# Cross-attention and feed-forward kernel: queries' and output's products on scaled 16-bit planes

## The chip, the cores and the metric

The kernel runs on one core of a Trainium2 chip. Its time is the device time in microseconds of one execution, as the median of several runs. A core has five engines that run side by side and meet at semaphores: TensorE (PE, matrix products; PEld is its loading of the stationary operand), VectorE (DVE), ScalarE (ACT), GpSimd (POOL), and SyncE (SP), which here issues every DMA. Sixteen DMA engines move the data. SBUF is the working memory of 128 partitions; TensorE writes its results into PSUM, eight banks of 512 fp32 columns.

## What is computed

Two layers, each an attention-like part and a feed-forward part, on x (2 batches x 512 tokens x 1024) and a context ctx (2 x 1024 x 1024), in float32:

```
x += fake_quant(layernorm(x)) @ fake_quant(ctx)          # 8-bit levels, layer 0
h  = layernorm(x)
x += h @ W.T + b + 2 * lora(h, routing from the mean of h)
h  = layernorm(x)                                        # layer 1
q  = rope(h @ wq)      32 heads x 128
k, v = rope(ctx @ wk), ctx @ wv      8 heads x 128, each used by 4 query heads
x += softmax(q k / sqrt(128) + mask) v @ wo
h  = layernorm(x)
x += h @ W_up.T + lora of the expert that the gate picks
```

The products have to be close to float32. The kernel gets this from two planes: a value is stored as a high plane (rounded to the narrower type) and a low plane (value minus high plane), and a product is three: low x high, high x low, high x high (`mm3`, lines 42 to 45).

## The kernel before

All five engines have a program written out by hand, in fixed order; each instruction waits for semaphores that name the step it needs. An engine never runs ahead of an instruction that waits. The names in the trace are tiles; the lines are those of the kernel before.

**First stage, 0 to about 408 us.** In 64 steps `s` TensorE makes keys and values of both batches, 24 products of 512 columns a step, and between them layer 0's quantised product. VectorE and ScalarE finish each step, SP stores planes of k and v to scratch in HBM. ScalarE's work in a step ends with the copy of planes and, in some steps, the root for a layernorm.

**Second stage, about 408 to 545 us.** The feed-forward of layer 0 in tiles of 128 tokens, a layernorm for each tile (`layernorm`, L1175: VectorE's statistics, ScalarE's root at L1679, VectorE again), the transposes of h through PSUM (`h_turn`), its high plane by ScalarE (`h_hi`, L1729) and low plane by VectorE (`h_lo`, L1371), stored by SP to `h_scratch` and read back transposed as hTa, hTb, hTc (1 MB each part, fp32).

**Third stage, the loop over heads, p = 0 to 65, each with four windows w.** The 64 heads are 32 heads of two batches. In a window TensorE does a quarter of the next head's queries (`q_part`, 6 products), scores of one tile of 128 queries (`scores`, 6), a quarter of the output product of the head pair before (`wo_part`, 6), and in window 0 also the values' product of the head before (`values`, 24, from 16-bit planes pT and vsb). The order in a window is values, q_part, wo_part, scores; in window 0 the output part comes after the scores. Planes of the queries' and output's products are fp32 planes of reduced precision (F32R, 4 bytes): wqh, wql, hT, woh, wol, osb.

What the others do in a window: VectorE makes `p_lo` of one tile (L1524: two inputs in SBUF), the row scale, the addition of the output product to x (`wo_add`, L1540), the maximum of the scores (L1507); in window 0 the low plane of the head's output (`o_lo`, L1529). After window 3 it applies the rope to the next queries (`q_end`, L1499). ScalarE makes the exponential (L1846), the high plane of the probabilities (`p_hi`, L1853), the cast of one slice of weights (`split_w`, L1805), in window 0 the cast of the head's output (`o_hi`, L1861), after window 3 that of the queries (`q_hi`, L1839). GpSimd has the low plane of the same slice (`split_w`, L1996) and the sum and low plane of the queries (`q_lo`, L2000 and L2002). SP issues the four loads of slices of the iteration (`load_w`, L601, 256 KB each, into four slots, each freed by the subtraction L1996), and in each window a transposing DMA of probabilities (`turn_p`, L625). `p_hi` of a tile waits for the transpose of the tile three before.

The first output product of an even p needs `o_lo` of the head before, the one just computed (L1022):

```
            if i == 0:
                e.wait_ge(p_wlo.sem, p_wlo[W_AT["o", q, 1]])
                e.wait_ge(v_olo.sem, v_olo[2 * j + 1])
```

Of the kernel before, what the change touches and what calls it, by code (L numbers as in the profile page):

```python
# [103 lines left out]
W_SLOT = [n % 4 if n < 250 else 2 + n % 2 for n in range(len(W_ORDER))]  # L104
# [6 lines left out]
UP_ON_DVE = [2, 3]  # L111
UP_LOAD_AT = {(62, 0): 0, (62, 1): 1, (62, 2): 2, (62, 3): 3, (63, 0): 4, (63, 3): 5, (64, 0): 6, (64, 1): 7}


def build_in(nc, ctx, A, out):
# [10 lines left out]
    h_d = nc.dram_tensor("h_scratch", [2, 128, 4, 2, 2, 512], F32, kind="Internal").ap()  # L126
# [15 lines left out]
    vsc = alloc(ctx, "vsc", [128, 24])  # L142

    x_lo = alloc(ctx, "x_lo", [128, 4, 1024])
# [11 lines left out]
    t_sb = alloc(one, "t_sb", [128, 512])  # L156
    khl = alloc(one, "khl", [128, 2, 2, 512], F32R)
# [27 lines left out]
    hTb = alloc(two, "hTb", [128, 4, 2, 2, 128], F32R)  # L185
    woh = alloc(two, "woh", [128, 2, 2, 512], F32R)
# [7 lines left out]
    osb = alloc(two, "osb", [128, 3, 2, 512], F32R)  # L194
    hTc = alloc(two, "hTc", [128, 4, 2, 2, 128], F32R)
# [102 lines left out]

    def w_dst(key, hl):
# [78 lines left out]
    t_rt = signal("t_rt", range(2))  # L378
# [25 lines left out]
    v_h2 = signal("v_h2", range(8))  # L404
    v_rt = signal("v_rt", [(b, j) for b in range(2) for j in range(8)])
# [26 lines left out]
    a_h2 = signal("a_h2", range(8))  # L432
    a_rt = signal("a_rt", range(2))
# [20 lines left out]
    p_qlo = signal("p_qlo", heads)  # L454
    v_up = signal("v_up", UP_ON_DVE)
# [5 lines left out]
    d_const = {n: signal(f"d_{n}", [n], 16) for n in ("cosk", "sink", "identf", "identb", "onesb", "scal", "bias", "rw",  # L461
                                                      "rb", "cosq", "sinq", "ag", "lb", "eb")}
# [6 lines left out]
    d_ar = [signal(f"d_ar{r}", [n for n in range(len(W_ORDER)) if W_SLOT[n] == r], 16) for r in range(4)]  # L469
# [5 lines left out]
    d_r3 = [signal(f"d_r3{r}", [k for k in range(8) if UP_SLOT[k] == r], 16) for r in range(3)]  # L475
# [26 lines left out]
    def sync_program(e):  # L502
# [21 lines left out]
        load("cosk", cosk[:, :])  # L524
        load("sink", sink[:, :])
# [8 lines left out]
        load("onesb", onesb[:, :])  # L534
        for group in steps():
# [55 lines left out]
        def store_h(tile):  # L591
            b, i = tile // 4, tile % 4
            for j in range(2):
                e.wait_ge(v_klo.sem, v_klo[tile, j])
                e.dma_start(h_d[b, :, i, j, :, :], f32(khl[:, j, :, :])).then_inc(d_khl[j].sem, 16)

        def load_w(key):
# [3 lines left out]
            e.dma_start(araw[:, W_SLOT[n], :], w_src(key)).then_inc(d_ar[W_SLOT[n]].sem, 16)  # L601

        def load_h(b, w):
            e.wait_ge(d_khl[w // 2].sem, d_khl[w // 2]["h", 4 * b + 3])
            e.dma_start(f32(hT_part(w)), h_d[b, :, :, w // 2, :, w % 2 * 256:w % 2 * 256 + 256].rearrange(
# [42 lines left out]

        e.wait_ge(t_kv.sem, t_kv[63])
        weights_split(e)  # L650
        for n in range(4):
            load_w(("q", n))
        for i in range(4):
            store_h(i)
            if i == 1:
# [8 lines left out]
        store_h(4)  # L664

# [15 lines left out]
        load("cosq", cosq[:, :])  # L681
        load("sinq", sinq[:, :])
# [15 lines left out]
        for p in range(66):  # L698
            if p % 4 == 0:
                load_k(p // 4 + 1)  # L700
            if 0 < p and 2 * p + 6 < 128:
                load_w(("q", 2 * p + 6))
            if has_wo(p + 1) and p < 62:
                load_w(("o", p + 1, 0))
                load_w(("o", p + 1, 1))
            if 0 < p and 2 * p + 7 < 128:
                load_w(("q", 2 * p + 7))
            for w in range(4):
# [8 lines left out]
                if 61 <= p <= 63 and w == 2:  # L717
                    load_w(("o", p + 2, 0))
                    load_w(("o", p + 2, 1))
# [44 lines left out]
    def tensor_program(e):  # L764
# [65 lines left out]

        def ffn_turn(tile):
# [17 lines left out]
        def router_end(b):  # L849
            e.wait_ge(v_rt.sem, v_rt[b, 2])  # L850
            if b == 0:
                e.wait_ge(d_const["rw"].sem, 16)
                e.wait_ge(d_const["rb"].sem, 16)
# [8 lines left out]
        for group in steps():  # L862
# [8 lines left out]
            if s in FFN_TURN_AT:  # L871
                ffn_turn(FFN_TURN_AT[s])
        def lora_t(b):
# [142 lines left out]
        def wo_part(q, i):  # L1016
# [145 lines left out]
    def vector_program(e):  # L1162
# [12 lines left out]
        def layernorm(key, x, dst):  # L1175
# [25 lines left out]
        def kv_end(s):  # L1201
# [907 lines left out]
```

## Time and profile before

| | us |
|---|---|
| median of 3 runs (lowest, highest) | 2078.19 (2078.07, 2079.86) |
| profiled execution, first to last instruction (span) | 2076.3 |
| around the span, to the median | 1.9 |
| mean granted TensorE clock | 0.997 of full speed |

The runs have no time of the profiled execution apart from its span, so the difference between span and median stands for what lies around it.

The page's second part cuts the span into 40 slices of 52 us; each digit is a busy share in tenths:

```profile
PE   8999999999899999999999999999999999999899
DVE  5887786667678877878878788888787877878744
ACT  3432341222365655565555555565555555655400
POOL 1552362511133343443434433334344343342400
```

TensorE is at nine tenths in nearly all of them. Slices 1 to 8 are the first stage, 9 to 11 the second and the start of the heads, 12 to 37 the loop. VectorE runs at seven to eight tenths in the loop. In the rows further down, a line such as "1000.33 0.39 PE L45 MATMUL" has the start, the duration, the engine, the line of the kernel and the operation; then output and inputs, shapes and types, and in brackets the idle time before it with what ended it. Matmuls overlap, so the time between two starts is the pace, not the duration.

### The profile page before, as it was taken

The numbers are of one execution on the slowest core, as the hardware profiler recorded it, in microseconds if no ns is written. First come the engines' busy times: TensorE is split into PE (matmuls) and PEld (weight loads), VectorE is DVE, ScalarE is ACT, GpSimd is POOL, SyncE is SP. The second block draws the span as 40 slices with busy tenths as digits, with TensorE's granted clock in tenths as the row PEclk, the third lists the DMA queues.
The fourth block names the chain that finished last, engine by engine and source line by source line (L and its number), as shares of the span: only waits on it lengthen the run. The fifth ranks groups of instructions, "written<-read, shape, count | busy, mean of one in ns | idle before, by whom it ended". The sixth has DMA issues, their size and how long they took to land.

```text
span 2076.3 us, 25530 instructions
## 1 busy us (share of the span) xinstructions
PE 2023.1 (97%) x9112; PEld 1520.3 (73%) x9116; DVE 1575.3 (76%) x2880; ACT 1002.6 (48%) x1418; POOL 747.1 (36%) x495
## 2 busy tenths in 40 slices
PE   8999999999899999999999999999999999999899
PEld 6877777887667777777777776777777777777587
DVE  5887786667678877878878788888787877878744
ACT  3432341222365655565555555565555555655400
POOL 1552362511133343443434433334344343342400
PEclk9999999999999999999999999999999999999999
DMA  7543553312978688786887899878687786777712
GB/s 267 171 162 122 186 170 102 133 60 101 325 173 172 140 185 168 148 178 137 190 165 146 198 237 235 192 149 184 141 181 165 151 183 142 172 161 142 206 61 72
DMA packets 654942, 341.11 MB, mean 164 GB/s; under 512 B 574720, under 2 KB 591360, under 8 KB 652768
## 3 DMA queue, kind: packets, MB, share of 16 engines
q1 hardware_dynamic: 654816, 339.48, 67.9%
q8 instruction: 73, 1.20, 0.2%
q14 instruction: 53, 0.43, 0.1%
HBM read 152.76 MB, written 44.04 MB: 95 GB/s over the span
## 4 chain that ended last, share of the span: by engine, by line
PE 78%; DVE 6%; DMA 3%; issue 2%; POOL 2%; ACT 1%; SPq 1%; DVEq 0%; ACTq 0%; POOLq 0%
PE ps L43 26%; PE ps L45 25%; PE ps L44 25%; DMA pT<-pp 1%; PE ps L820 1%; POOL u_sb L1960 1%; DVE t_sb L1164 1%; DVE pp L1524 1%; DVE psb L1507 1%; DMA raw<-in_ctx 0%; SPq L625 0%; DMA sinq<-in_sinq 0%; PE ps L1060 0%; PE ps L1044 0%; PE ps L827 0%
## 5 line engine op out<-in xcount | busy, mean ns | idle before, releaser
L1846 ACT ACTIVATE psb<-psb,st 128x1024 f32<-128x1024 f32 x256 | 295.1, 1153 | 220.7 <-DVE st L1510 220.5
L1524 DVE SCALAR_TENSOR_TENSOR pp<-psb,st,pp 128x1024 f16<-128x1024 f32 x256 | 380.9, 1488 | 5.1 <-ACT pp L1853 3.0
L1507 DVE CUSTOM_DVE_ANT_0 psb<-ps,mask 128x1024 f32<-128x1024 f32 x256 | 313.5, 1224 | 84.7 <-PE ps L45 77.9
L1853 ACT ACTIVATE pp<-psb,st 128x1024 f16<-128x1024 f32 x256 | 293.7, 1147 | 144.9 <-DVE st L1519 143.8
L1996 POOL TENSOR_TENSOR wol<-araw,woh 128x512 fp32r<-128x512 f32 x128 | 167.6, 1310 | 431.9 <-ACT woh L1805 431.8
L1996 POOL TENSOR_TENSOR wql<-araw,wqh 128x512 fp32r<-128x512 f32 x128 | 165.3, 1292 | 331.6 <-ACT wqh L1805 331.6
L1164 DVE TENSOR_TENSOR x_lo<-ps,x_lo 128x512 f32<-128x512 f32 x264 | 181.0, 686 | 51.8 <-PE ps L45 51.8
L43 PE MATMUL ps<-woh,osb 128*128 128x512 f32 x512 | 202.6, 396 | 9.3 <-DVE x_lo L1164 4.1
L43 PE MATMUL ps<-ksb,qsb 128*128 128x512 f32 x512 | 200.5, 392 | 7.5 <-DVE st L1507 4.5
L44 PE MATMUL ps<-wol,osb 128*128 128x512 f32 x512 | 200.2, 391 | 0.0
L45 PE MATMUL ps<-woh,osb 128*128 128x512 f32 x512 | 200.2, 391 | 0.0
L45 PE MATMUL ps<-ksb,qsb 128*128 128x512 f32 x512 | 199.5, 390 | 0.0
L43 PE MATMUL ps<-pT,vsb 128*128 128x512 f16 x512 | 194.8, 380 | 4.9 <-DMA pT<-pp 4.9
L44 PE MATMUL ps<-ksb,qsb 128*128 128x512 f32 x512 | 199.5, 390 | 0.0
L45 PE MATMUL ps<-pT,vsb 128*128 128x512 f16 x512 | 194.1, 379 | 0.0
L44 PE MATMUL ps<-pT,vsb 128*128 128x512 f16 x512 | 194.1, 379 | 0.0
L43 PE MATMUL ps<-slots,wl 128*128 128x512 f32 x448 | 177.8, 397 | 11.4 <-ACT slots L1659 8.3
L45 PE MATMUL ps<-slots,wh 128*128 128x512 f32 x448 | 175.4, 392 | 0.0
L44 PE MATMUL ps<-slots,wh 128*128 128x512 f32 x448 | 175.1, 391 | 0.0
L2000 POOL TENSOR_TENSOR ua<-ua,ta 128x512 f32<-128x512 f32 x64 | 136.5, 2133 | 82.2 <-DVE ta L1164 82.2
L1839 ACT CAST qsb<-ua 128x512 fp32r<-128x512 f32 x64 | 39.7, 620 | 193.5 <-POOL ua L2000 193.5
L1529 DVE SCALAR_TENSOR_TENSOR osb<-ps,vsc,osb 128x512 fp32r<-128x512 f32 x64 | 48.1, 751 | 111.5 <-ACT osb L1861 111.5
(254 smaller groups left out, 4131.2 us busy)
## 6 DMA issues: line engine op xcount, KB each, us to landing
araw<-in_wq SPq DMA_DIRECT2D x128, 256.0 KB, 4.8
araw<-in_wo SPq DMA_DIRECT2D x128, 256.0 KB, 4.5
k_scratch<-khl SPq DMA_DIRECT2D x32, 512.0 KB, 3.6
ksb<-k_scratch SPq DMA_DIRECT2D x16, 1024.0 KB, 6.0
raw<-in_wv SPq DMA_DIRECT2D x16, 512.0 KB, 4.5
raw<-in_ctxT SPq DMA_DIRECT2D x16, 512.0 KB, 4.6
raw<-in_wk SPq DMA_DIRECT2D x16, 512.0 KB, 5.6
raw<-in_ctx SPq DMA_DIRECT2D x16, 512.0 KB, 4.6
```

Of the source, the lines that this page charges most:

```text
L43: e.matmul(dst, ll, rh, start=start, stop=False)
L44: e.matmul(dst, lh, rl, start=False, stop=False)
L45: return e.matmul(dst, lh, rh, start=False, stop=stop)
L1164: return e.tensor_tensor(dst, a, b, op)
L1507: e.tensor_tensor_reduce(out=psb[:, n % 3, :], in0=pair(n % 2 * 2), in1=mask[:, i, :], scale=1.0, scalar=LOWEST, op0=ALU.add, op1=ALU.max, ...
L1524: e.scalar_tensor_tensor(out=pp[:, r, 1024:2048], in0=psb[:, r, :], scalar=st[:, n // 4 % 4, 16 + i:17 + i], in1=pp[:, r, 0:1024], op0=ALU ...
L1529: e.scalar_tensor_tensor(out=osb[:, H % 3, 1, :], in0=bank(4), scalar=vsc[:, H // 4:H // 4 + 1], in1=f32(osb[:, H % 3, 0, :]), op0=ALU.mul ...
L1839: e.copy(qsb[:, H % 2, 0, :], ua[:, :]).then_inc(a_qhi.sem, 1)
L1846: e.activation(P, P, ACT.Exp, bias=c[:, 4 + i:5 + i], accum_out=c[:, 8 + i:9 + i]).then_inc(a_exp.sem, 1)
L1853: e.activation(pp[:, r, 0:1024], psb[:, r, :], ACT.Copy, scale=st[:, n // 4 % 4, 16 + i:17 + i]).then_inc(a_ph.sem, 1)
L1996: e.tensor_tensor(w_dst(key, 1), araw[:, W_SLOT[n], :], f32(w_dst(key, 0)), ALU.subtract).then_inc(p_wlo.sem, 1)
L2000: e.tensor_tensor(ua[:, :], ua[:, :], ta[:, :], ALU.add).then_inc(p_qu.sem, 1)
```

## The change

- The planes of queries' and output's products (wqh, wql, hT, woh, wol, osb) become float16. The tiles keep their places in SBUF.
- Float16 has a small range, so weights are scaled by a power of two first. The power comes from the sum of squares of all of wq and of all of wo. 128 slices of 512 columns are loaded ahead of time (`load_square`, SP), squared and summed by ScalarE (`square`), added over partitions by three small fp32 products (`square_sums`, TensorE), and turned into scales by short chains on VectorE (`query_sums`, `query_scale`, `value_squares`, `output_sums`, `output_scales`). 64 slices (wq) fall into steps 6 to 59 of the first stage, 64 (wo) into the second stage, between ScalarE's pieces there.
- GpSimd multiplies every raw slice by its scale in place (`scale_w`), called one slice ahead at the start of `split_w`; ScalarE's cast waits for that.
- Raw slices get eight slots instead of four, and are loaded one iteration earlier. At p = 0 SP now has four loads ahead of the first `turn_p` of the loop, where it had none.
- cosq and sinq are multiplied by the inverse scale before the first rope, the layernorm of h by 1024, and the addition of the output product multiplies it by its inverse scale.
- Some semaphores of constants are shared, and h_scratch has half its bytes.

The core of the diff:

```
-W_SLOT = [n % 4 if n < 250 else 2 + n % 2 for n in range(len(W_ORDER))]
+W_SLOT = [n % 4 if n < 8 else n % 8 if n < 248 else 2 + (n - 248) % 6 for n in range(len(W_ORDER))]
+SQUARE_STEPS = sorted([*range(6, 28), *range(38, 60), *range(40, 60)])
+H_SCALE = 1024.0
...
-    wqh = alloc(two, "wqh", [128, 3, 512], F32R)
-    wql = alloc(two, "wql", [128, 3, 512], F32R)
+    wqh = alloc(two, "wqh", [128, 3, 512], F16)
+    alloc(two, "wqh_pad", [128, 1536], F16)
+    wql = alloc(two, "wql", [128, 3, 512], F16)
+    alloc(two, "wql_pad", [128, 1536], F16)
...
+        def load_square(n):
+            if n > 6:
+                e.wait_ge(a_sq.sem, a_sq[n - 7])
+            w = A["wq" if n < 64 else "wo"][n // 2 % 32]
+            e.dma_start(scan[:, n % 7, :], w[:, n % 2 * 512:n % 2 * 512 + 512]).then_inc(d_scan[n].sem, 16)
...
         for p in range(66):
             if p % 4 == 0:
                 load_k(p // 4 + 1)
-            if 0 < p and 2 * p + 6 < 128:
-                load_w(("q", 2 * p + 6))
-            if has_wo(p + 1) and p < 62:
-                load_w(("o", p + 1, 0))
-                load_w(("o", p + 1, 1))
-            if 0 < p and 2 * p + 7 < 128:
-                load_w(("q", 2 * p + 7))
+            if 2 * p + 8 < 128:
+                load_w(("q", 2 * p + 8))
+            if p < 64:
+                load_w(("o", p + 2, 0))
+                load_w(("o", p + 2, 1))
+            if 2 * p + 9 < 128:
+                load_w(("q", 2 * p + 9))
...
+        def square_sums(what):
+            if what == "w":
+                e.wait_ge(v_scal.sem, v_scal[0])
+                e.wait_ge(a_sq.sem, a_sq[63])
+                e.wait_ge(v_l0.sem, v_l0[1, 6, 0])
+                e.matmul(ps[:, 7, 0:64], twos[:, :], squares[:, 0:64], start=True, stop=True).then_inc(t_rt.sem, 1)
+            else:
+                e.wait_ge(a_sq.sem, a_sq[127])
+                e.wait_ge(v_ws.sem, v_ws["v", 1])
+                e.wait_ge(v_qr.sem, v_qr[0])
+                e.matmul(ps[:, 7, 0:64], twos[:, :], squares[:, 64:128], start=True, stop=True)
+                e.matmul(ps[:, 7, 64:80], twos[:, :], sc[:, 32:48], start=True, stop=True).then_inc(t_rt.sem, 1)
...
+        def query_sums():
+            e.wait_ge(t_rt.sem, t_rt["w"])
+            e.tensor_reduce(sc[:, 0:1], ps[:, 7, 0:64], AX, ALU.add).then_inc(v_ws.sem, 1)
+            bound(1, "w", 0)
...
         split_lo("c21")
+        query_sums()
+        query_scale()
         row_sums(1)
...
+                e.tensor_scalar(cosq[:, :], cosq[:, :], sc[:, 18:19], None, ALU.mult).then_inc(v_ws.sem, 1)
+                e.tensor_scalar(sinq[:, :], sinq[:, :], sc[:, 18:19], None, ALU.mult).then_inc(v_ws.sem, 1)
...
-            tt(xs, bank(6 + i % 2), xs, ALU.add).then_inc(v_xa.sem, 1)
+            e.scalar_tensor_tensor(out=xs, in0=bank(6 + i % 2), scalar=sc[:, 30 + (q - 2) // 32:31 + (q - 2) // 32], in1=xs,
+                                   op0=ALU.mult, op1=ALU.add).then_inc(v_xa.sem, 1)
...
+                if (p, w) == (0, 1):
+                    output_sums()
+                    output_scales()
...
+        def square(n):
+            e.wait_ge(d_scan[n].sem, d_scan[n]["s", n])
+            e.activation(scan[:, n % 7, :], scan[:, n % 7, :], ACT.Square, accum_out=squares[:, n:n + 1]).then_inc(a_sq.sem, 1)
...
         ffn_hi(4)
+        for n in range(72, 75):
+            square(n)
         root(("f", 6))
...
+        ffn_hi(5)
+        for n in range(76, 84):
+            square(n)
+        root(("f", 7))
         split_w(("q", 0))
...
+        for n in range(125, 128):
+            square(n)
         split_w(("q", 3))
...
+        def scale_w(n):
+            if n < len(W_ORDER):
+                wo, r = W_ORDER[n][0] == "o", W_SLOT[n]
+                e.wait_ge(d_ar[r].sem, d_ar[r][n])
+                if n == 0:
+                    e.wait_ge(v_ws.sem, v_ws["w", 5])
+                if wo and n < 12:
+                    e.wait_ge(v_ws.sem, v_ws["v", 8])
+                e.tensor_scalar(w_raw(n), w_raw(n), sc[:, 16 + wo:17 + wo], None, ALU.mult).then_inc(p_ws.sem, 1)
+
         def split_w(key):
             n = W_AT[key]
+            scale_w(n + 1)
             e.wait_ge(a_whi.sem, a_whi[n])
-            e.tensor_tensor(w_dst(key, 1), araw[:, W_SLOT[n], :], f32(w_dst(key, 0)), ALU.subtract).then_inc(p_wlo.sem, 1)
+            e.tensor_tensor(w_dst(key, 1), w_raw(n), w_dst(key, 0), ALU.subtract).then_inc(p_wlo.sem, 1)
```

## Rows read from the trace of the kernel before

**Rows 1.** The page, busy us (share of the span) xinstructions:
```profile
PE 2023.1 (97%) x9112; PEld 1520.3 (73%) x9116; DVE 1575.3 (76%) x2880; ACT 1002.6 (48%) x1418; POOL 747.1 (36%) x495
```
**Rows 2.** Busy time by stretch: us, then each engine, clock, DMA:
```profile
640.00:1900.00 1260.00, 1253.70 (x5556) 912.64 (x5555) 1011.98 (x1852) 735.99 (x1042) 500.98 (x346) 1.00 0.80 171
```
**Rows 3.** TensorE in order of time, a 32-bit run, then values' products:
```profile
1000.33 0.39 PE L45 MATMUL ps<-hTb,wqh 128*128 128x512 f32 x1
...
1007.13 0.39 PE L45 MATMUL ps<-ksb,qsb 128*128 128x512 f32 x1
...
1007.59 0.38 PE L44 MATMUL ps<-pT,vsb 128*128 128x512 f16 x1
...
1012.12 0.38 PE L44 MATMUL ps<-pT,vsb 128*128 128x512 f16 x1
```
**Rows 4.** TensorE, last scores product and first output product of an even p:
```profile
1079.69 0.39 PE L45 MATMUL ps<-ksb,qsb 128*128 128x512 f32 x1
1080.20 0.47 PE L43 MATMUL ps<-woh,osb 128*128 128x512 f32 x1
```
**Rows 5.** All engines in order of time, ahead of that output product:
```profile
1075.65 1.28 DVE L1524 SCALAR_TENSOR_TENSOR pp<-psb,st,pp 128x1024 f16<-128x1024 f32 x1
...
1075.70 2.38 POOL L2000 TENSOR_TENSOR ua<-ua,ta 128x512 f32<-128x512 f32 x1 [1.14 <-DVE ta L1164]
...
1078.63 0.68 ACT L1861 ACTIVATE osb<-ps,vsc 128x512 fp32r<-128x512 f32 x1
...
1079.35 0.75 DVE L1529 SCALAR_TENSOR_TENSOR osb<-ps,vsc,osb 128x512 fp32r<-128x512 f32 x1 [2.15 <-ACT osb L1861]
```
**Rows 6.** The same view, windows 2 and 3 of the iteration before:
```profile
1063.86 1.29 POOL L1996 TENSOR_TENSOR wol<-araw,woh 128x512 fp32r<-128x512 f32 x1 [3.16 <-ACT woh L1805]
...
1065.36 1.27 DVE L1524 SCALAR_TENSOR_TENSOR pp<-psb,st,pp 128x1024 f16<-128x1024 f32 x1
...
1068.87 1.30 POOL L1996 TENSOR_TENSOR wol<-araw,woh 128x512 fp32r<-128x512 f32 x1 [3.72 <-ACT woh L1805]
...
1069.44 1.81 DVE L1524 SCALAR_TENSOR_TENSOR pp<-psb,st,pp 128x1024 f16<-128x1024 f32 x1
```
**Rows 7.** Groups by line: xcount, busy us, mean ns, idle before:
```profile
L1996 POOL TENSOR_TENSOR wql<-araw,wqh 128x512 fp32r<-128x512 f32 x128 | 165.3, 1292 | 331.6 <-ACT wqh L1805 331.6
...
L1164 DVE TENSOR_TENSOR x_lo<-ps,x_lo 128x512 f32<-128x512 f32 x264 | 181.0, 686 | 51.8 <-PE ps L45 51.8
...
L1529 DVE SCALAR_TENSOR_TENSOR osb<-ps,vsc,osb 128x512 fp32r<-128x512 f32 x64 | 48.1, 751 | 111.5 <-ACT osb L1861 111.5
...
L1839 ACT CAST qsb<-ua 128x512 fp32r<-128x512 f32 x64 | 39.7, 620 | 193.5 <-POOL ua L2000 193.5
...
L1679 ACT ACT_TABLE_LOAD x4 | 5.1, 1283 | 0.1
```
**Rows 8.** All engines in order of time, first stage:
```profile
74.25 2.96 DVE L1197 TENSOR_SCALAR tmp<-x_lo,sm 128x1024 f32<-128x1024 f32 x1
74.28 2.39 POOL L1952 TENSOR_TENSOR wl<-raw,wh 128x1024 fp32r<-128x1024 f32 x1
```
**Rows 9.** SP's issues, GpSimd and ScalarE in order of time, p = 0:
```profile
564.21 15.95 SPq L625 DMA_TRANSPOSE pT<-pp  x4
...
572.03 1.89 POOL L1996 TENSOR_TENSOR wql<-araw,wqh 128x512 fp32r<-128x512 f32 x1 [4.32 <-ACT wqh L1805]
...
575.71 1.15 ACT L1853 ACTIVATE pp<-psb,st 128x1024 f16<-128x1024 f32 x1
```
**Rows 10.** DMA issues, 640 to 1900 us: count, median us to landing:
```profile
pT<-pp SPq DMA_TRANSPOSE x232, 4.3
```
**Rows 11.** A small VectorE operation; ScalarE's root ahead of tile 7:
```profile
397.62 0.15 DVE L1228 TENSOR_SCALAR vsc<-vsc 128x1 f32<-128x1 f32 x1
...
473.28 0.20 ACT L1679 ACTIVATE sm<-sm 128x1 f32<-128x1 f32 x1 [8.15 <-DVE sm L1183]
```
**Rows 12.** TensorE in order of time, start of the second stage:
```profile
415.17 0.47 PE L43 MATMUL ps<-slots,h2s 128*128 128x512 f32 x1 [1.61 <-DVE slots L1164]
```

More of the change, by code:

```diff
@@ L111 @@
 UP_ON_DVE = [2, 3]
+SQUARE_STEPS = sorted([*range(6, 28), *range(38, 60), *range(40, 60)])
+SQUARE_LOAD_STEP = [max(SQUARE_STEPS[n - 7] + 1 if n > 6 else 0, SQUARE_STEPS[n] - 2) for n in range(64)]
+SQUARES = range(128)
+H_SCALE = 1024.0
 UP_LOAD_AT = {(62, 0): 0, (62, 1): 1, (62, 2): 2, (62, 3): 3, (63, 0): 4, (63, 3): 5, (64, 0): 6, (64, 1): 7}
@@ L142, in build_in @@
     vsc = alloc(ctx, "vsc", [128, 24])
+    vso = alloc(ctx, "vso", [128, 16])
+    twos = alloc(ctx, "twos", [128, 128])
+    squares = alloc(ctx, "squares", [128, 128])
+    sc = alloc(ctx, "sc", [128, 64])
+    more = ExitStack()
+    araw2 = alloc(more, "araw2", [128, 4, 512])
+    more.close()
+    scan = alloc(ctx, "scan", [128, 7, 512])
     x_lo = alloc(ctx, "x_lo", [128, 4, 1024])
@@ L404, in build_in @@
     v_h2 = signal("v_h2", range(8))
+    v_ws = signal("v_ws", [("w", j) for j in range(7)] + [("v", j) for j in range(2)] + ["cosq", "sinq"]
+                  + [("v", j) for j in range(2, 12)])
     v_rt = signal("v_rt", [(b, j) for b in range(2) for j in range(8)])
@@ L580, in sync_program @@
                 load_raw(f"x{C_LOAD_AT[s]}")
+            for m in range(64):
+                if SQUARE_LOAD_STEP[m] == s:
+                    load_square(m)
         load_raw("c20")
@@ L646, in load_up @@
             e.dma_start(raw3(k), A["up"][k]).then_inc(d_r3[UP_SLOT[k]].sem, 16)
+        for n in range(64, 71):
+            load_square(n)
         e.wait_ge(t_kv.sem, t_kv[63])
@@ L652, in sync_program @@
             load_w(("q", n))
+        for n in range(71, 105):
+            load_square(n)
         for i in range(4):
             store_h(i)
+            for n in (range(105, 110), range(110, 116), range(116, 120), range(120, 125))[i]:
+                load_square(n)
             if i == 1:
@@ new lines, in output_sums, with output_scales @@
+        def output_sums():
+            e.wait_ge(t_rt.sem, t_rt["v"])
+            e.tensor_reduce(sc[:, 0:1], ps[:, 7, 0:64], AX, ALU.add).then_inc(v_ws.sem, 1)
+            e.tensor_reduce(sc[:, 1:3], ps[:, 7, 64:80].rearrange("p (a b) -> p a b", a=2), AX, ALU.add).then_inc(v_ws.sem, 1)
+            bound(3, "v", 3)
+        def output_scales():
+            floor_roots(3, "v", 5)
+            e.tensor_scalar(sc[:, 17:18], sc[:, 12:13], 2.0 ** 14, None, ALU.mult).then_inc(v_ws.sem, 1)
+            e.tensor_scalar(sc[:, 20:22], sc[:, 13:15], 2.0 ** 13, None, ALU.mult).then_inc(v_ws.sem, 1)
+            e.tensor_scalar(sc[:, 30:32], sc[:, 10:12], sc[:, 9:10], 2.0 ** -27, ALU.mult, ALU.mult).then_inc(v_ws.sem, 1)
+            e.wait_ge(v_ws.sem, v_ws["v", 9])
+            for b in range(2):
+                m = e.tensor_scalar(vso[:, 8 * b:8 * b + 8], vsc[:, 8 * b:8 * b + 8], sc[:, 20 + b:21 + b], None, ALU.mult)
+            m.then_inc(v_ws.sem, 1)
@@ L1775, in scalar_program @@
                 root(("f", FFN_NORM_AT[s]))
+            for n in range(64):
+                if SQUARE_STEPS[n] in group:
+                    square(n)
         split_hi("c20")
@@ L1787, in scalar_program @@
         lora_hi(0)
+        for n in range(64, 72):
+            square(n)
         def split_w(key):
             n = W_AT[key]
-            e.wait_ge(d_ar[W_SLOT[n]].sem, d_ar[W_SLOT[n]][n])
+            e.wait_ge(p_ws.sem, p_ws[n])
             if key[0] == "q":
@@ L2004, in gpsimd_program @@
         bias(6)
+        scale_w(0)
         bias(7)
```

154 lines of the change are left out of this document (111 added, 43 removed).

## The prediction

> **What bounds the kernel now.** I read the page first: TensorE is busy 97% of the span, VectorE 76%, ScalarE 48%, GpSimd 36% [rows 1]. Then the busy times by stretch: from 640 to 1900 us, in the loop over heads, TensorE has 1253.7 of 1260 us at granted clock 1.00, VectorE 1012, GpSimd 501 [rows 2]. So the loop, 61% of the time, goes at the pace of matmuls, and an edit counts there if it shortens matmuls or makes TensorE wait. Then TensorE in order of time, start to start: 30 steps of products on 32-bit planes from 1000.33 to 1007.13 us give 0.2267 us each, 21 steps of 16-bit ones (values) from 1007.59 to 1012.12 give 0.2157 [rows 3]. A product of 512 columns is thus 0.0110 us cheaper on 16-bit planes. The durations printed there overlap; I don't use them.
> Last, what TensorE still waits for. An iteration (one head) lasts 21.54 or 21.92 us by turns; the longer one has a wait ahead of its first output product, from 1079.69 to 1080.20 where 0.227 is due, with 0.08 in the next step [rows 4]: 0.37 us, in 26 of the 29 even iterations between 640 and 1900. Its cause stands in four rows [rows 5]: VectorE starts `p_lo` (L1524, two SBUF inputs) at 1075.65, GpSimd starts the query addition (L2000) 0.05 later and takes 2.38 us, 1.1 more than its like in [rows 6]; the query cast waits for that, ScalarE's cast of the head's output stands behind it (1078.63), then VectorE's low plane of the output (1079.35 to 1080.10), then the product. GpSimd and VectorE's operations with two SBUF inputs exclude one another. This chain decides what the change is worth.
>
> **The change part by part.** The sum is made against the profiled execution: span 2076.3, and 1.9 us around it make the median of 2078.2.
> *Matmuls.* 64 heads x 24 of the queries and as many of the output go to 16-bit planes: 3072 x 0.0110 = 33.8 us. The 72 of heads 0 to 2 and the 96 of the last four output steps lie where TensorE waits for others anyway; without them 31.9. The order query, output, scores now changes kind in every window: from 1007.13 to 1007.59 one 32-bit and one first 16-bit step take 0.46 where 0.442 would be due [rows 3]; over all 63 such places I read 0.0115 a change. Three more 16-bit runs in each of 61 iterations lose 183 x 0.0115 = 2.1. Term: -29.8 us (bounds -33.8 and -27).
> *GpSimd's scaling (`scale_w`)*, 252 operations of 128x512, four an iteration. The trace has no GpSimd operation with one tensor input; the nearest is the subtraction with two, 1.29 us [rows 7], the upper bound; the lower is half of it, 0.65, if half the reads are half the time. I take 0.8, nearer the lower, as reads are what differs. As busy time it is free: 3.2 us on an engine busy 8.6 of 21.7. But it stands right behind each subtraction, and `p_lo` comes there. Today, in window 2, the subtraction ends at 1065.15 and `p_lo` starts at 1065.36, unhindered; in window 3 it starts inside the subtraction, takes 1.81 instead of 1.27 and so begins when GpSimd is done [rows 6]. Who goes first when both come at once: with 0.03 us between the stamps GpSimd won, and 0.8 us of VectorE took 2.96 [rows 8]; with 0.05 VectorE won [rows 5]. No row has a second GpSimd operation queued while VectorE waits; I expect VectorE to get in.
> Stepped forward from an output product at 0, with halves of 1.29 and scores of 1.36 us: window 0's subtraction ends at 2.0, scaling at 2.8, `p_lo` is due at 2.2, ends 0.4 late. Window 1's scores end at 5.25, so the next `p_lo` is due at 6.8 in any case; ScalarE, 0.4 late, has let the subtraction run to 7.2: 0.2 late. Window 2: due at 10.7, subtraction to 11.6, 0.65 late, as today. The head's rope starts 0.15 us late. When the race at 2.2 costs 0.9, the same steps give 0.6. Cover ahead of the output product (query and scores products) shrinks by 0.06, so the wait of the even iterations becomes 0.6 to 1.0 us for 0.37. Term: +0.4 x 31 = +12 us (bounds 0 and +44, under the rivals).
> *VectorE in the loop.* The addition of the output product turns into a scaled one: 0.686 now, 0.751 for the like operation with a pointer scalar [rows 7]; 0.065 x 4 an iteration, inside the steps above. ScalarE's casts and all low planes keep their element counts: 0 (bounds -0.1 and +0.1 us each, off the path except for the head's output, +-3 in all).
> *Loads.* Slices come one iteration earlier into eight slots; in the steady loop SP waits for the same subtraction as now: 0. At iteration 0 four loads are new ahead of SP's `turn_p(1)`, issued today at 564.21; the last waits for slice 7's subtraction, ended at 573.9 [rows 9]. The transpose lands 4.3 us [rows 10] after about 575, and `p_hi(4)`, at 575.71 today [rows 9], waits for it, near 4 us. Slices already there take part of this back later on: +1.5. The output's scales add 12 small VectorE operations there, each 0.15 [rows 11] and 0.04 to the next: 2.3 us, of which 1.0 counts.
> *Squares.* 128 loads of 256 KB and 128 ScalarE squares of 512 columns: a cast of that size is 0.62 [rows 7], 0.75 with the sum's read-out, 96 us in all. Up to 408 us they stand last in a step of 5.4 us, one or two each, where ScalarE idles: 0. From 443 to 545 they fill its waits, as eight of them the 8.15 us ahead of the root at 473.28 [rows 11]. +0.5 where they don't fit; if they don't hide, +8.
> *Ahead of the heads.* `query_sums` and `query_scale`, eight small VectorE operations of 0.19, stand before low planes of W's slices, for which TensorE already waits at 415.17 [rows 12]: +1.5. Scaling cosq and sinq +0.9, given back by halved stores of h in the same chain. Three small fp32 products +0.3. This and the two paragraphs before: +5 (bounds -2 and +14).
> Together -29.8 + 12 + 5 = -12.8: 2065.4.
> The Trainium skill (GPSIMD Engine Reference, Engine selection) has one-input operations on GpSimd at roughly line rate, while two-input ones are about twice as slow as VectorE's; no row here shows it. By it `scale_w` would be near 0.6, the +12 near +8, and the sum 2061.
>
> **The rivals.**
> *The port costs nothing:* `p_lo` never loses to a scaling. The wait is 0.37 + 0.06: 2078.2 - 29.8 + 2 + 4 = 2054. For it: GpSimd idles 60% of the loop [rows 2]; against: the 0.21 us between subtraction and `p_lo` [rows 6].
> *Just cancelled:* `scale_w` takes 1.29 like the subtraction. A race is lost in every iteration, the wait becomes 1.0 to 1.1, and a transpose comes 0.1 late to the values: +0.8 x 31 = 25, in all 2078.
> *Slower:* GpSimd keeps the port from subtraction to scaling while VectorE waits. Then `p_lo` loses 0.6 to 1.2 in two or three windows, rope is 1.0 late, the output product waits 1.3, and window 2's transposes reach the values 0.4 and 0.1 late: 1.8 a pair of iterations for 0.37, +1.43 x 31 = 44; 2078.2 - 29.8 + 44 + 5 = 2097. It decides from 1.0 us of extra wait a pair. [Rows 8] speaks for it, the 1.81 in [rows 6] against.
> *The squares don't stay in their cover:* they need another function table than the root. Loads of a table take 1.28 us and stand at changes between root and exponential [rows 7]; with squares between, each of ten roots from 457 to 540 us waits for one, on the path of VectorE's layernorm. Two thirds of 12.8 us reach TensorE: +9, 2074. The Trainium skill (ScalarE: Activation LUTs, Table sets: the hidden batching unit) names relu, copy, identity and abs as part of every set and not the square; by it the loads come if the root's set lacks it.
>
> **How the numbers follow.** Forecast 0.50, port free 0.17, cancelled 0.14, slower 0.12, tables 0.07. The time is the first's, 2065. The range goes from 2048, below the port-free case since GpSimd could also come to win the race of [rows 5] and end today's 0.37 x 26, to 2085, which leaves out the slower case and little else. A measurement can tell 0.2%, 4.2 us, from no change. Faster (under 2074.0): 0.44 of the forecast's 0.50, port free, half of tables: 0.65. Same: the forecast's rest, half of tables, most of cancelled: 0.17. Slower: 0.18.
>
> **What would show it.** Steps of query and output products at 0.216; iterations without a wait at 21.0 us. The wait ahead of the first output product in even iterations: 0.43 is the port-free case, 0.6 to 1.0 mine, 1.3 with waits for pT the slower one. The duration of `scale_w`; how many `p_lo` take 1.27, 1.8 or more; table loads between 443 and 545; when the values' first product starts. I am wrong if 16-bit products beside 32-bit ones don't keep 0.216, or if waits for slices or masks appear.

## The result and the profile after

The changed kernel takes 2065.89 us (median of 5 runs, 2063.38 to 2070.57) where the kernel before took 2078.19 beside it (2078.01 to 2082.31): 0.9945 of it, 95% interval 0.9933 to 0.9958. The forecast was 2065. The profiled execution has a span of 2061.6 against 2076.3, 14.7 us less. That sum came out right although two of its terms were wrong, by about as much in opposite directions.

Two stamps divide the trace: the first product on the second head's values, and that of the 62nd. Columns: start in us, duration, engine, line, operation, tiles, shapes, count, idle time and its releaser. Before:
```profile
594.24 0.38 PE L43 MATMUL ps<-pT,vsb 128*128 128x512 f16 x1 [2.12 <-DMA pT<-pp]
...
1900.32 0.39 PE L43 MATMUL ps<-pT,vsb 128*128 128x512 f16 x1
```
After:
```profile
608.53 0.38 PE L43 MATMUL ps<-pT,vsb 128*128 128x512 f16 x1 [0.73 <-DMA pT<-pp]
...
1886.01 0.39 PE L43 MATMUL ps<-pT,vsb 128*128 128x512 f16 x1
```
The way to the first stamp became 14.3 us longer. The 60 iterations between them take 1277.5 for 1306.1 us, 28.6 less (periods of 21.15 and 21.45 by turns, for 21.54 and 21.93). What is behind takes 175.6 for 176.0.

The page's busy line, which is of the whole span, and the loop's row answer to [rows 1, 2]:
```profile
PE 2001.8 (97%) x9118; PEld 1235.3 (60%) x9122; DVE 1599.0 (78%) x2903; ACT 1080.4 (52%) x1674; POOL 1266.2 (61%) x751
```
```profile
640.00:1900.00 1260.00, 1252.86 (x5675) 665.36 (x5674) 1061.30 (x1895) 752.74 (x1064) 996.29 (x589) 1.00 0.81 172
```
TensorE is as full as before, at the same granted clock of 1.00 (2.4 GHz). GpSimd is busy twice as long, 996 for 501 us, and nobody waits for it more than before. The products of queries and output now go at the 16-bit pace (against [rows 3]): eleven steps from the first row to the second take 2.38 us, 0.216 each, and that is the median step inside these runs over the whole loop, where it was 0.227.
```profile
1000.19 0.38 PE L43 MATMUL ps<-hTa,wql 128*128 128x512 f16 x1
...
1002.57 0.38 PE L45 MATMUL ps<-woh,osb 128*128 128x512 f16 x1
```
The chain ahead of an even iteration's first output product is that of [rows 4, 5], no longer than it was:
```profile
1036.97 1.28 DVE L1658 SCALAR_TENSOR_TENSOR pp<-psb,st,pp 128x1024 f16<-128x1024 f32 x1
1037.02 2.36 POOL L2185 TENSOR_TENSOR ua<-ua,ta 128x512 f32<-128x512 f32 x1 [1.22 <-DVE ta L1239]
...
1040.66 0.75 DVE L1663 SCALAR_TENSOR_TENSOR osb<-ps,vso,osb 128x512 f16<-128x512 f32 x1 [2.14 <-ACT osb L2035]
...
1041.51 0.38 PE L43 MATMUL ps<-woh,osb 128*128 128x512 f16 x1 [0.17 <-issue]
```
18 iterations between 620 and 1890 us have such a step, of 0.56 us where 0.22 is due: 0.34 lost. Before, 26 lost 0.37, the step behind it included. I had forecast 0.6 to 1.0 in 31.

By line, shapes apart (columns: count, busy us, mean ns, idle before), against [rows 7]:
```profile
L2175 POOL TENSOR_SCALAR araw<-araw,sc 128x512 f32<-128x512 f32 x256 | 563.2, 2200 | 51.9 <-DMA araw<-in_wq 51.9
L2181 POOL TENSOR_TENSOR wol<-araw,woh 128x512 f16<-128x512 f32 x128 | 149.0, 1165 | 109.4 <-ACT woh L1953 109.4
...
L1876 ACT ACTIVATE scan<-scan 128x512 f32<-128x512 f32 x128 | 79.3, 624 | 0.0
L1876 ACT ACTIVATION_READ_ACCUMULATOR scan<-scan 128x1 f32 x128 | 24.4, 191 | 0.0
L1817 ACT ACT_TABLE_LOAD x4 | 5.1, 1283 | 0.1
```
The scaling takes 2.20 us, far above my upper bound of 1.29; alone it is 1.56 (91 of 256), in the other cases it stands behind VectorE and is stamped with 2.5 to 2.6. The subtraction went from 1.29 to 1.17 with its 16-bit result. Table loads are four at the root and eight in all, as before: the squares needed none. The Trainium skill (ScalarE: Activation LUTs, Table sets: the hidden batching unit) has relu, copy, identity and abs in every set and doesn't name the square among them; here the square caused no load either, beside root, exponential and copy, and the rival of the table loads fell.

**Where the 14.3 us arise.** The last rope additions of stage 1, before and then after, show that 8.7 of the 14.3 were there already:
```profile
407.77 2.32 POOL L1960 TENSOR_TENSOR u_sb<-u_sb,t_sb 128x512 f32<-128x512 f32 x1 [0.92 <-DVE t_sb L1164]
```
```profile
416.46 2.33 POOL L2134 TENSOR_TENSOR u_sb<-u_sb,t_sb 128x512 f32<-128x512 f32 x1 [0.93 <-DVE t_sb L1239]
```
Of the 8.7, 5.0 had come by the rope addition that was at 297 us before, 2.7 more come by that of 318, none from there to that of 382, and 1.0 at that of 388. One link of the stretch around 300 us, in time order, before:
```profile
298.59 0.62 ACT L1667 CAST khl<-u_sb 128x512 fp32r<-128x512 f32 x1 [5.04 <-POOL u_sb L1960]
299.12 1.05 ACT L1659 CAST wh<-raw 128x1024 fp32r<-128x1024 f32 x1
...
301.99 0.68 DVE L1164 TENSOR_TENSOR u_sb<-ps,cosk 128x512 f32<-128x512 f32 x1
...
307.92 2.13 POOL L1972 TENSOR_TENSOR ctab<-ctab,bq 128x1024 f16<-128x1024 f16 x1
310.10 0.60 PE L807 MATMUL ps<-ctab,onesb 128*128 128x512 f16 x2 [1.41 <-POOL ctab L1972]
```
The same stretch after:
```profile
304.13 0.63 ACT L1805 CAST khl<-u_sb 128x512 fp32r<-128x512 f32 x1 [4.36 <-POOL u_sb L2134]
304.66 0.63 ACT L1876 ACTIVATE scan<-scan 128x512 f32<-128x512 f32 x1
305.29 0.62 ACT L1876 ACTIVATE scan<-scan 128x512 f32<-128x512 f32 x1
305.90 1.04 ACT L1797 CAST wh<-raw 128x1024 fp32r<-128x1024 f32 x1
306.97 1.23 DVE L1239 TENSOR_TENSOR wl<-raw,wh 128x1024 fp32r<-128x1024 f32 x1 [2.32 <-ACT wh L1797]
308.12 0.68 DVE L1239 TENSOR_TENSOR u_sb<-ps,cosk 128x512 f32<-128x512 f32 x1
...
314.01 2.13 POOL L2146 TENSOR_TENSOR ctab<-ctab,bq 128x1024 f16<-128x1024 f16 x1
...
316.19 1.03 PE L863 MATMUL ps<-ctab,onesb 128*128 128x512 f16 x2 [4.90 <-POOL ctab L2146]
```
Two squares stand between the casts. "Last in a step" is first in the next one for an engine that works in order: the weight cast comes 6.8 us after its like of before instead of 5.5, VectorE's low plane waits 2.32 us for it, rope and the context's table follow 6.1 us late, and TensorE waits 4.90 us instead of 1.41. The granted clock falls with it, from 1.00 to 0.91 as the mean of 20 us. Rows of 300 to 320 us, before and then after (columns: window; busy us of PE, PEld, DVE, ACT, POOL, then clock, DMA share, GB/s):
```profile
300.00:320.00 20.00, 18.59 (x89) 14.85 (x88) 14.79 (x27) 6.86 (x11) 9.78 (x6) 1.00 0.47 158
```
```profile
300.00:320.00 20.00, 15.10 (x60) 11.83 (x59) 16.05 (x30) 11.59 (x26) 11.71 (x7) 0.91 0.78 245
```
The second thing to see there is the share of the DMA engines, 0.78 for 0.47.

### The profile page after: what moved, and what is told of

It reads as the page before. It is cut to its first block, busy times and chain, and to the rows that moved or that the text cites. A ratio compares the mean times of both kernels' runs of the same rounds, so it can differ in the third digit from the quotient of the medians.

```text
span 2061.6 us, 26211 instructions
## 1 busy us (share of the span) xinstructions
PE 2001.8 (97%) x9118; PEld 1235.3 (60%) x9122; DVE 1599.0 (78%) x2903; ACT 1080.4 (52%) x1674; POOL 1266.2 (61%) x751
## 4 chain that ended last, share of the span: by engine, by line
PE 77%; DVE 6%; DMA 3%; issue 2%; ACT 2%; POOL 2%; SPq 0%; ACTq 0%; DVEq 0%; POOLq 0%
PE ps L43 25%; PE ps L45 24%; PE ps L44 24%; PE ps L876 1%; POOL u_sb L2134 1%; DMA pT<-pp 1%; DVE t_sb L1239 1%; DMA raw<-in_ctx 1%; DVE pp L1658 1%; DVE psb L1641 0%; DVE vhl_sb L1311 0%; ACT wh L1797 0%; DVE u_sb L1239 0%; PE ps L1133 0%; PE ps L883 0%
## 5 line engine op out<-in xcount | busy, mean ns | idle before, releaser
L2175 POOL TENSOR_SCALAR araw<-araw,sc 128x512 f32<-128x512 f32 x256 | 563.2, 2200 | 51.9 <-DMA araw<-in_wq 51.9
L1658 DVE SCALAR_TENSOR_TENSOR pp<-psb,st,pp 128x1024 f16<-128x1024 f32 x256 | 400.3, 1564 | 3.5 <-ACT pp L2027 1.5
L43 PE MATMUL ps<-ksb,qsb 128*128 128x512 f32 x512 | 250.8, 490 | 9.5 <-DVE st L1641 6.9
L2181 POOL TENSOR_TENSOR wol<-araw,woh 128x512 f16<-128x512 f32 x128 | 149.0, 1165 | 109.4 <-ACT woh L1953 109.4
L43 PE MATMUL ps<-woh,osb 128*128 128x512 f16 x512 | 195.0, 381 | 9.2 <-issue 4.8
L45 PE MATMUL ps<-ksb,qsb 128*128 128x512 f32 x512 | 203.0, 396 | 0.0
L44 PE MATMUL ps<-ksb,qsb 128*128 128x512 f32 x512 | 202.6, 396 | 0.0
L1674 DVE SCALAR_TENSOR_TENSOR x_lo<-ps,sc,x_lo 128x512 f32<-128x512 f32 x256 | 190.4, 744 | 14.0 <-PE ps L45 12.8
L45 PE MATMUL ps<-woh,osb 128*128 128x512 f16 x512 | 194.7, 380 | 0.0
L44 PE MATMUL ps<-wol,osb 128*128 128x512 f16 x512 | 194.5, 380 | 0.0
L2181 POOL TENSOR_TENSOR wql<-araw,wqh 128x512 f16<-128x512 f32 x128 | 149.8, 1170 | 55.3 <-ACT wqh L1953 55.3
L44 PE MATMUL ps<-slots,wh 128*128 128x512 f32 x448 | 175.6, 392 | 0.0
L45 PE MATMUL ps<-slots,wh 128*128 128x512 f32 x448 | 175.6, 392 | 0.0
L2134 POOL TENSOR_TENSOR u_sb<-u_sb,t_sb 128x512 f32<-128x512 f32 x32 | 50.1, 1566 | 153.2 <-DVE t_sb L1239 153.2
```

Of the source, the lines that this page charges most:

```text
L43: e.matmul(dst, ll, rh, start=start, stop=False)
L44: e.matmul(dst, lh, rl, start=False, stop=False)
L45: return e.matmul(dst, lh, rh, start=False, stop=stop)
L1658: e.scalar_tensor_tensor(out=pp[:, r, 1024:2048], in0=psb[:, r, :], scalar=st[:, n // 4 % 4, 16 + i:17 + i], in1=pp[:, r, 0:1024], op0=ALU ...
L1674: e.scalar_tensor_tensor(out=xs, in0=bank(6 + i % 2), scalar=sc[:, 30 + (q - 2) // 32:31 + (q - 2) // 32], in1=xs, op0=ALU.mult, op1=ALU.a ...
L2134: e.tensor_tensor(u, u, t_sb[:, :], ALU.add).then_inc(p_ku.sem, 1)
```

## Experiments

All are compared with the kernel before on the same chip in turn (medians of 2079 to 2080 us there, where it was 2078 beside the result). "Lag" is the start of a stamp less its start in the trace before: at 408 us the last rope addition, at 594 us the second head's values. Each lag is of one trace. Up to 408 us experiments 4, 8 and 12 are the changed kernel, and where that has a lag of 8.7, they have 7.0, 6.8 and 11.2; 8 and 12 are it up to 594 us, too, with 11.5 and 16.3 for 14.3. So a difference of 2 or 3 us between two traces can be scatter. The stretch between the two stamps of the loop is 1277.5 to 1281.2 us in all traces with the change but that of experiment 12. Medians from different chips are best compared by their ratios.

**1. Neither squares nor loads.** `load_square` and `square` do nothing; `squares` is filled with a constant; waits for `a_sq` fall.
```
 def square(n):
-    e.wait_ge(d_scan[n].sem, ...); e.activation(... ACT.Square ...)
+    pass
```


> The changed kernel without the 128 squares on ScalarE and without their 128 loads; the sums that the scales come from are a constant, everything behind them stays. Measured so far: the second head's first value product starts 14.3 us later after the change than before (8.7 us of it by 408 us, while the contexts' keys and values are made). Theory A (squares on ScalarE): ScalarE works in order, and two squares of 0.62 + 0.19 us at the end of a step push its casts and contexts' quantisation; without them 10 to 12 of the 14.3 us go, time 2054 to 2056. Theory B (SP and DMA): the same gain here, but it must come back in the run with loads alone. Theory C (the new small operations ahead of the heads and the scalings): under 3 us go, 2063 or more.

Measured: 2050.53 us, ratio 0.9859 [0.9843, 0.9874]; lag 1.4 us at 408, 2.2 at 594. More came back than I had expected. In the traces the squares and their loads cost 12.1 of the 14.3 us, and all else that the change adds ahead of the second head some 2. Between the medians it is more, as the trace of this run is its slowest execution (2054.77) and that of the changed kernel its fastest (2063.38). The loop is no faster than that after the change (1281.2 us between the stamps).

**2 and 3. Loads alone, squares alone.** In 2 each load waits for the one seven earlier and no square runs. In 3 all squares read one slice.
```
-e.wait_ge(a_sq.sem, a_sq[n - 7])
+e.wait_ge(d_scan[n - 7].sem, d_scan[n - 7]["s", n - 7])        # 2
-e.activation(scan[:, n % 7, :], scan[:, n % 7, :], ACT.Square, ...)
+e.activation(scan[:, 1 + n % 6, :], scan[:, 0, :], ACT.Square, ...)   # 3
```


> The changed kernel with the 128 loads of 256 KB in their places (each waits for the landing of the one seven before, not for its square) but no square on ScalarE; the sums are a constant. Theory A: as without both, 2054 to 2057, and the lag at 408 us under 1.5 us. Theory B (the loads stand ahead of the raw slices' loads on SP, and take the DMA engines): the lag at 408 us stays above 6 us, time 2062 to 2066.

> The changed kernel with its 128 squares on ScalarE in their places, all of one slice loaded once, written into six places by turns; the other 127 loads are left out. Theory A: as the changed kernel, 2063 to 2066, lag at 408 us 7 to 9 us. Theory B: 2054 to 2057, lag under 2 us. If both this and the loads alone keep about half, the two add up: a square waits for its late load and ScalarE stands behind it.

Measured: 2059.17 (0.9895 [0.9879, 0.9911]), lags 6.0 and 8.5; and 2060.10 (0.9900 [0.9885, 0.9915]), lags 5.0 and 9.9. Neither theory alone: with 2050.5 for none and 2065.9 for both, the loads cost 8.7, the squares 9.6, and together 15.4, a little less than the sum. (Experiment 4, on the same chip in turn and with all loads and squares, stands for both at 2065.95.)

**4. No scaling in the loop.** `scale_w` isn't called; the query tables' and output's scales are set to fit.
```
 def split_w(key):
-    scale_w(n + 1)
```


> The changed kernel without GpSimd's 256 scalings of weight slices (2.2 us each as profiled, 563 us of GpSimd): the slices go to 16-bit planes unscaled, and the scales of the query tables and the output are set to fit. Loop from the second to the 62nd head's value products: 1277.5 us with them. Theory A (VectorE gets in between subtraction and scaling, and the delays end inside the cover ahead of the output product): 1275 to 1278 without, time 2062 to 2066. Theory B (my term of +12 is there, and the matmuls gave more than I counted): 1264 to 1267, time 2051 to 2055.

Measured: 2065.95 (0.9927 [0.9913, 0.9940]), the changed kernel's time by the medians and 0.0018 or 3.7 us under it by the ratios, which are as uncertain as that; between the stamps 1281.2 us, not less. GpSimd's busy time halves and TensorE's stays:
```profile
640.00:1900.00 1260.00, 1251.98 (x5667) 663.50 (x5664) 1032.86 (x1893) 750.10 (x1062) 480.51 (x353) 1.00 0.81 172
```
The longer step ahead of the first output product is there without any scaling, too, in 22 iterations for 18. So my +12 isn't there: 563 us of GpSimd cost nothing that these runs can tell.

**5. Small loads.** Experiment 2 with 64 of each 512 columns: as many issues, an eighth of the bytes.
```
-e.dma_start(scan[:, n % 7, :], w[:, c0:c0 + 512])
+e.dma_start(scan[:, n % 7, 0:64], w[:, c0:c0 + 64])
```


> The run with loads alone, each load cut from 128x512 to its first 64 columns (32 KB for 256 KB); as many DMA issues on SP, in the same places; no square on ScalarE, sums a constant. Loads alone took 2059.2 us against 2050.5 without loads and squares, and its lag at 408 us was 6.0 us against 1.4. Theory bytes (the squares' loads take the DMA engines from the raw slices, whose landing TensorE's operands wait for): 2050 to 2053, lag under 2.5 us. Theory issue (SP's order: each issue keeps SP from the raw slices' loads): 2057 to 2060, lag above 4.5 us.

Measured: 2050.14 (0.9857 [0.9844, 0.9870]), lag -1.4 us at 408. It is the bytes, not the issues. The landing of a raw slice, with the loads whole and then small (KB each, median us from issue to landing; 5.6 before the change, 5.9 after):
```profile
raw<-in_wk SPq DMA_DIRECT2D x16, 512.0 KB, 6.2
```
```profile
raw<-in_wk SPq DMA_DIRECT2D x16, 512.0 KB, 4.8
```
Without any of these loads it is 5.5 (experiment 1). That small ones come out under none, here and in experiment 10 (4.7), stays unexplained.

**6, 7 and 9. Fewer squares, other places.** In 6 and 9 half of the slices are loaded and squared, and counted twice; in 7 all of them, and the loads move with the squares. The lines of the diff that set the places:
```
+SQUARE_STEPS = sorted([*range(51, 59)] * 3 + [*range(59, 63)] * 2)              # 6, half
+SQUARE_STEPS = sorted([*range(24, 36), *range(38, 51), 48, 49, 50]
+                      + [*range(51, 63)] * 3)                                   # 7, all
+SQUARE_STEPS = sorted([*range(47, 51)] * 2 + [*range(51, 59)] * 3)              # 9, half
```


> The changed kernel with half of the squares: of each of the 64 slices of 1024 columns only the first 512 go into the sums, counted twice (the scale, a power of two, then rests on half of the weights; the rest of the computation is whole). The 32 of the query weights all stand in steps 51 to 62 (327 to 400 us), where the full set added no lag, the 32 of the output weights where half of them stood. Theory A (cost follows the place: none between 327 and 388 us, and half of the 4 to 5 us of the part after 408): 2052 to 2055. Rival (three squares and loads a step no longer fit beside the casts and the raw slices there): 2058 to 2062.

> The changed kernel, all 128 squares, but none in steps 6 to 23: one each in steps 24 to 35 and 38 to 47, two in 48 to 50, three in 51 to 62. Theory A (loads ahead of 150 us meet the busiest raw loads, and the first lag of 2 to 3 us stays): lag at 408 us 8.7 us becomes 3 to 5, time 2060 to 2063. Rival (the places are as good as each other, the lag goes with the number): 2064 to 2067.

> As the run with half of the squares, but the 32 of the query weights stand in steps 47 to 58 (two in 47 to 50, three in 51 to 58) and so end before 385 us. That run took 2057.4 us and TensorE waited 5.05 us at 407.7 for the product over the squares, against 1.02 at the same place without squares. Theory A (that wait was the late last squares, and the places themselves cost nothing): wait under 1 us, time 2053 to 2055. Rival (the cost goes with their number in any place): 2056 to 2059.

Measured: 2057.44 (0.9892 [0.9878, 0.9907]); 2070.57 (0.9956 [0.9945, 0.9967]); 2056.65 (0.9879 [0.9864, 0.9894]). All three missed what I had expected of theory A (at most 2055, 2063 and 2055). In experiment 7 the lag at 240 us is -0.8 as hoped (2.6 after the change), but 6.1 at 408, and there TensorE waits in order for the last squares' sums, as it does in experiment 6, whose last sum is read out at 407.62:
```profile
407.72 0.61 PE L893 MATMUL ps<-squares,twos 128*128 128x32 f32 x2 [5.05 <-issue]
```
(5.66 us in 7.) Experiment 9 takes this wait away, and its median is only 0.8 us lower. Its lag at 408 is 3.1 against 1.1 in experiment 6, but that is no price of its places: 1.3 against -0.6 stood at the rope addition of 297 us, ahead of the first square of either. From there both lose the same: 0.2 us up to the addition of 382, with three squares a step, and 1.6 at that of 388. Experiment 7, too, stands at 4.5 from 318 to 382 and loses 1.6 at 388. So the places between 318 and 382 us were free at that density as well, and the ones just behind them weren't. What experiment 7 lost ahead of them came at 252 us (2.3) and between 297 and 318 (2.6).

**8 and 12. More work for GpSimd.** A second operation behind each scaling of slices 16 to 247.
```
+e.tensor_scalar(w_raw(n)[:, 0:256], w_raw(n)[:, 0:256], one, None, ALU.mult)   # 8
+e.tensor_tensor(dump(n), w_raw(n), w_raw(n), ALU.add)                          # 12
```


> The changed kernel with a second GpSimd multiplication of half a slice (128x256, by 1.0) behind each scaling of slices 16 to 247. Theory A (GpSimd's operations and VectorE's with two SBUF inputs exclude one another, and VectorE gets in between two): per iteration GpSimd 4 x (1.56 + 1.17) + 1.3 + 1.3 = 13.5, VectorE's low planes 4 x 1.27 = 5.1, together 18.6 of 21.3 us, which is why the scaling costs nothing; 3.1 more plus four waits makes some 22.1, over the 21.3: period 22 to 22.8, time +40 to +85 us, 2105 to 2150. Rival (they share, GpSimd has 5 us to spare): period 21.3 to 21.5, time under 2078.

> The changed kernel with a GpSimd addition of the slice to itself (two inputs, 128x512, into memory that nothing reads) behind each scaling of slices 16 to 247. In the trace after the change VectorE's low plane of P that comes 0.03 to 0.22 us after a scaling starts ends its delay 0.49 us after that start (15 of 15), one that comes inside the subtraction 0.97 us after it (158): a one-input operation of 1.56 us holds the other engine off for 0.49, a two-input one of 1.16 for 0.97. Theory A (it is the holds that reach TensorE, not GpSimd's busy time): the addition, 1.2 us and so less GpSimd time than 0.93 + 0.6, but with holds of 0.97 in every window where the half multiplication had 0.28, delays more of VectorE's low planes; loop +0.2 to +0.8 us an iteration, time 2078 to 2115. Rival (VectorE's slack of 16% takes that too): within 3 us of the changed kernel.

Measured: 2065.13 (0.9932 [0.9919, 0.9944]) and 2090.42 (1.0051 [1.0039, 1.0064]). GpSimd's operations by line in the loop, first of 8, then of 12:
```profile
L2177 POOL TENSOR_SCALAR araw<-araw,sc 128x512 f32<-128x512 f32 x235 | 394.8, 1680 | 0.0
...
L2181 POOL TENSOR_SCALAR araw<-araw,sc 128x256 f32<-128x256 f32 x230 | 212.8, 925 | 21.5
...
L2192 POOL TENSOR_TENSOR ua<-ua,ta 128x512 f32<-128x512 f32 x59 | 127.2, 2156 | 12.6 <-DVE ta L1240 11.9
```
```profile
L2179 POOL TENSOR_SCALAR araw<-araw,sc 128x512 f32<-128x512 f32 x233 | 366.2, 1572 | 0.0
L2184 POOL TENSOR_TENSOR osb_pad<-araw 128x512 f32<-128x512 f32 x231 | 287.5, 1245 | 19.3
...
L2195 POOL TENSOR_TENSOR ua<-ua,ta 128x512 f32<-128x512 f32 x58 | 130.9, 2257 | 0.3 <-DVE ta L1243 0.2
```
Experiment 8 refutes the budget that I had drawn up (all of GpSimd's time and `p_lo`'s added, 22.1 us): they overlap. The two added operations differ little alone, 0.93 and 1.04 us, but in 8 nothing is lost (GpSimd is busy for 1181 of the 1260 us there), in 12 some 0.4 us an iteration. In 12 GpSimd hasn't a moment left ahead of the query addition (0.3 us of idle time for 12.6) and starts it 0.9 late in nearly every iteration, on the chain to the output product. Longer holds (below) and a full GpSimd act together there; the runs don't part them, though the price fell in the range of theory A.

**10 and 11. An eighth of the columns.** All loads and squares in their places, 64 columns each; in 11 only the output weights'. The scales then rest on an eighth of the weights.
```
+c = 64                       # 11: 64 if n > 63 else 512
+e.dma_start(scan[:, n % 7, 0:c], w[:, c0:c0 + c])
+e.activation(scan[:, n % 7, 0:c], ..., ACT.Square, scale=(512 / c) ** 0.5, accum_out=...)
```


> The changed kernel with all 128 loads and squares in their places, but each of the first 64 of its 512 columns only, multiplied by the square root of 8 before the square (the scale, a power of two, then rests on an eighth of the weights; all else is whole): 32 KB a load, and a short ScalarE operation. Theory A (the cost is bytes on the DMA engines and ScalarE's time per column; not issues, waits, sums or the scales themselves): 2050 to 2054, lag at 408 us under 2.5 us; both kernels are beaten. Rival (part of the cost is a fixed time per square in ScalarE's order, 0.4 us x 128): 2056 to 2060.

> The changed kernel with the output weights' 64 squares and loads cut to 64 columns as in the run above, the query weights' 64 whole. Theory A (the part after 408 us loses 4 to 5 us by the output weights' squares): lag at 408 us 7 to 9, as after the change, then no more than 1.5 us more up to the second head's values; time 2060 to 2062. Rival (what is lost after 408 comes from the lag before it, by transfers that then stand elsewhere): 2064 to 2067.

Measured: 2052.25 (0.9862 [0.9849, 0.9876]), lags -0.2 and -1.3; and 2061.55 (0.9913 [0.9899, 0.9927]), lags 9.1 and 10.8. Experiment 10 beats both kernels: 128 squares, with a fixed 0.19 us of sum read-out and 0.25 us of work each, hide where 0.62 and 256 KB don't. By the medians experiment 11 puts 4.3 us on the output weights' half and 9.3 on the queries'. The traces agree on the first: from 408 to 594 us the lag grows by 1.7 us in 11, and by 4.7 to 6.8 in the four traces with whole ones there (5.6 after the change).

## Why the prediction was right, and where it wasn't

*What bounds the kernel.* Right: the loop goes at the pace of matmuls before and after.

*Matmuls, -29.8.* Right. For the 60 iterations measured the step gives 60 x (48 x 0.0110 - 3 x 0.0115) = 29.6; they gained 28.6. By the scatter of the other traces the gain is 25 to 29, so up to 5 us of it can have gone to VectorE's longer addition, the scaling and the rest together. No experiment undoes the 16-bit planes by themselves; the term rests on the pace of their steps, 0.216 for 0.227.

*GpSimd's scaling, +12.* Failed; experiment 4 shows no cost, with room for some 4 us. The duration was off upwards (1.56 us alone, where I had taken 0.8 and allowed 1.29), and its effect downwards, and I had tied the two together. Both orders can be read in the trace after. VectorE waits for the subtraction, then GpSimd's scaling for VectorE:
```profile
1064.39 1.16 POOL L2181 TENSOR_TENSOR wql<-araw,wqh 128x512 f16<-128x512 f32 x1
...
1064.83 1.79 DVE L1658 SCALAR_TENSOR_TENSOR pp<-psb,st,pp 128x1024 f16<-128x1024 f32 x1
...
1065.53 2.53 POOL L2175 TENSOR_SCALAR araw<-araw,sc 128x512 f32<-128x512 f32 x1
```
`p_lo`, alone 1.27, ends 1.27 after 1065.35, 0.97 after the subtraction's start; the scaling, queued behind, ends 1.4 us after `p_lo`. So VectorE gets in, as I had expected, and the rival in which GpSimd keeps the port fell. So did the one that just cancels: its 1.29 us for a scaling is nearer than mine, its +25 isn't there. It gets in 0.2 us before the subtraction's end, so there is no race with the scaling behind it. The same stood in [rows 6], where I had read that `p_lo` begins when GpSimd is done: 1069.44 + 1.81 - 1.27 is 1069.98, and the subtraction ends at 1070.17. The Trainium skill (GPSIMD Engine Reference, Engine selection) expects a one-input operation near line rate; the trace has it slower (1.56 us) than the two-input subtraction of the same size (1.17). The port-free rival, 2054, had the loop right, and experiment 1, without the squares' cost, comes near it with 2050.5.

*Squares, +0.5 (+8 if they don't hide).* Failed: 12.1 us in the traces, 15.4 between the medians, above even the second figure. I had weighed ScalarE's idle time by step, not what comes next in its order, and for the loads I had looked at SP's order and not at the engines that carry them. Experiments 2, 3 and 5 show both halves.

*Loads of iteration 0, output scales, query scale: about +4.5, the rest of the +5.* Together 2.2 in the trace of experiment 1, and nothing in those of 5 and 10, whose lags at 594 us are -2.5 and -1.3.

*The sum* held since +12 that wasn't there stood for 12 that were elsewhere. Measured in the traces: -28.6, +14.3, -0.4. That two errors are of one size is chance; only the matmul term was measured as forecast.

## What to carry to other kernels

Work that is put into an engine's idle time costs what stands next in that engine's order, so look at the successor's chain, not at the busy share; and the price of a prefetch was its bytes beside the transfers that an engine waits for, not its issues (experiment 5). When several traces of one stretch of code exist, their scatter comes first: experiment 9's lag looked like a price and stood there before its first square. Cutting the bytes and columns of a statistic (experiment 10) took away what moving it about (7, 9) did not. A check of each term by its own stretch of the trace, not of the total, tells whether a forecast was right.

## What the runs showed of the hardware

The time for which GpSimd holds VectorE's two-SBUF-input operation off isn't the duration that its own operation is stamped with. In all 15 places where `p_lo` started 0.03 to 0.22 us after a scaling of 1.56 us, its delay ended 0.49 to 0.50 us after the scaling's start (a start 0.03 after it cost 0.46); two that started 0.95 and 1.25 after it weren't delayed. A two-input subtraction of 1.16 us held it for 0.97. How much of a stamped duration GpSimd spends on reading, no trace shows. In experiment 8 the half multiplication runs on while `p_lo` takes its undisturbed time:
```profile
1062.05 0.93 POOL L2181 TENSOR_SCALAR araw<-araw,sc 128x256 f32<-128x256 f32 x1
...
1062.37 1.27 DVE L1660 SCALAR_TENSOR_TENSOR pp<-psb,st,pp 128x1024 f16<-128x1024 f32 x1
```
An operation that GpSimd starts inside `p_lo` waits for its end and then takes nearly all its time: 164 scalings are stamped with 2.5 to 2.6 us and end 1.35 to 1.44 us after `p_lo`. With only 0.05 us between the stamps either can win: `p_lo` did in 47 of 59 query additions after the change, GpSimd in 12 (48 and 10 before).
